# An FFN schedule that starts three stages later inside a Runge-Kutta scan

## The reference, cut to what matters

```
def _derivative(q, p, drive, coupling, bias):
    i_couple = jnp.tanh(q) @ coupling.T
    dq = q - q ** 3 / 3.0 - p + drive + i_couple + bias
    dp = EPSILON * (q + ALPHA - BETA * p)
```

```
gate_up = jnp.einsum('bsh,oh->bso', x, w_gu)
h = jax.nn.silu(gate) * up
y = jnp.einsum('bsi,hi->bsh', h, w_down)
rms = jnp.sqrt(jnp.mean(y * y, axis=-1, keepdims=True) + EPS)
```

## Time and profile before

| | |
|---|---|
| median of 3 runs | 1503.43 us (1503.01 to 1503.76) |
| the profiled execution | 1503.53 us |
| its span in the trace | 1501.7 us |
| PE busy | 1429.6 us (95%) |
| PEld busy | 1399.2 us (93%) |
| DVE busy | 1449.4 us (97%) |
| ACT busy | 719.2 us (48%) |

### The profile page before, as it was taken

How to read it: one execution, slowest core, us unless ns; L and a number is a source line. 1 busy time by engine, 2 the same in 40 slices (tenths; PEclk the granted TensorE clock), 3 DMA queues, 4 the chain that set the end, 5 groups by cost and what they waited for, 6 DMA issues and landing times.

```text
span 1501.7 us, 90826 instructions
## 1 busy us (share of the span) xinstructions
PE 1429.6 (95%) x37025; PEld 1399.2 (93%) x37025; DVE 1449.4 (97%) x11277; ACT 719.2 (48%) x4836; POOL 12.5 (1%) x39
## 2 busy tenths in 40 slices
PE   2477999999999999999999999999999999999998
PEld 0366999999999999999999999999999999999998
DVE  6999999999999999999999999999999999999991
ACT  2144445445454554545455454555455555545541
POOL 0000000000000000000000000000000000000000
PEclk9999999999999999999999999999999999999999
DMA  9200000000000000000000000000000000000000
GB/s 222 50 7 14 4 8 7 9 20 4 25 4 22 7 6 23 4 25 4 22 8 5 24 4 25 4 22 8 4 25 4 25 4 22 8 4 25 4 22 22
DMA packets 11942, 28.41 MB, mean 19 GB/s; under 512 B 1537, under 2 KB 5889, under 8 KB 11393
## 3 DMA queue, kind: packets, MB, share of 16 engines
q1 hardware_dynamic: 11522, 22.60, 6.0%
HBM read 18.40 MB, written 4.19 MB: 15 GB/s over the span
## 4 chain that ended last, share of the span: by engine, by line
PE 88%; DVE 8%; issue 0%; ACT 0%; POOLq 0%; DVEq 0%; POOL 0%; ACTq 0%
PE scan_ps L538 51%; PE gu_ps L301 22%; PE y_ps L313 14%; DVE th L610 1%; DVE q_stage L648 1%; DVE with_q L604 1%; DVE q_sq L614 1%; DVE scan_ps L622 1%; DVE q_stage L646 1%; DVE q_cub L617 1%; DVE p_part L604 1%; DVE with_p L604 0%; DVE q_raw L648 0%; DVE q_raw L646 0%; DVE hist L633 0%
## 5 line engine op out<-in xcount | busy, mean ns | idle before, releaser
L538 PE MATMUL scan_ps<-th,wscan 128*128 128x32 f16 (+1 forms) x32768 | 1006.1, 175 | 31.4 <-ACT th L576 31.1
L538 PEld LDWEIGHTS scan_ps<-th,wscan 128*128 128x128 f16 x32768 | 924.6, 96 | 49.1 <-ACT th L576 40.0
L576 ACT ACTIVATE th<-q_stage 128x16 f16<-128x16 f32 x1536 | 318.7, 207 | 524.3 <-DVE q_stage L646 524.3
L301 PE MATMUL gu_ps<-hist,wffn 128*128 128x128 f32 x2816 | 503.1, 284 | 0.0
L301 PEld LDWEIGHTS gu_ps<-hist,wffn 128*128 128x128 f32 x2816 | 393.8, 192 | 0.0
L610 DVE TENSOR_TENSOR th<-t,th 128x16 f16<-128x16 f32 x2048 | 357.9, 175 | 0.4 <-ACT t L578 0.2
L313 PE MATMUL y_ps<-wffn,h 128*128 128x128 f32 x1408 | 323.6, 313 | 0.0
L578 ACT ACTIVATE t<-q_stage 128x16 f32<-128x16 f32 x1536 | 306.2, 199 | 0.0
L313 PEld LDWEIGHTS y_ps<-wffn,h 128*128 128x128 f32 x1408 | 209.5, 189 | 0.4 <-DVE h L329 0.4
L576 ACT ACTIVATE th<-q_raw 128x16 f16<-128x16 f32 x512 | 106.2, 208 | 202.1 <-DVE q_raw L646 174.8
L379 ACT ACTIVATE sum_r<-dr,constant 128x64 f32<-128x64 f32 x528 | 174.3, 333 | 18.1 <-DMA dr<-drive 18.1
(11 more groups left out here) (36 smaller groups left out, 554.8 us busy)
## 6 DMA issues: line engine op xcount, KB each, us to landing
raw<-packed SPq DMA_DIRECT2D x11, 768.0 KB, 11.6
dr<-drive SPq DMA_DIRECT2D x34, 128.0 KB, 2.7
xres<-x SPq DMA_DIRECT2D x16, 256.0 KB, 3.5
out<-osb SPq DMA_DIRECT2D x16, 256.0 KB, 2.9
coup<-coupling_t SPq DMA_DIRECT2D x1, 1024.0 KB, 13.0
sc<-scales SPq DMA_DIRECT2D x1, 33.0 KB
q_raw<-cond_t SPq DMA_DIRECT2D x1, 16.0 KB, 5.6
bias<-bias_t SPq DMA_DIRECT2D x1, 2.0 KB, 6.2
```

The lines of the kernel that those rows point to most:

```text
L301: i = nc.tensor.matmul(gu_ps[b][:, half * P:(half + 1) * P], wffn[:, u, j * P:(j + 1) * P], hist[1 - f.parity][:, kt].rearrange("p t b -> ...
L538: i = nc.tensor.matmul(to if both else to[:, 0], wscan[:, w, part, kt, cols], moving if both else moving[:, 0], start=first, stop=last, sk ...
L576: nc.scalar.activation(th[s % 2][:, c, 0, :], q[:, c, :], ACT.Tanh, scale=1.0 / S).then_inc(now.tanh_hi, 1)
```

## The change

One number changes, and with it every stage at which the FFN has a job:

```
-FFN_FIRST = 0
+FFN_FIRST = 3
```

## The result

| | before | after |
|---|---|---|
| median of 6 runs each | 1503.8 us (1503.01 to 1504.88) | 1509.86 us (1509.34 to 1510.46) |
| ratio, 95% interval | | 1.0041 (1.003 to 1.0052) |
| profiled span | 1501.7 us | 1508.6 us |

The change costs 6.1 us, twice the 3.0 that were forecast, and the time lies above the predicted range.

A forecast was written before the change was run, and what follows sets the result against it. DVE was taken to end boundaries with two products, TensorE those with three. Blocks +1.1, start +0.1 and tail +1.8 us made 3.0 to 3.1 on 1503.53: 1506.5 us, put at 1506.4 against the median, range 1505.3 to 1507.8.

The forecast's parts named there:

- the block's sum of 0.08 us: Over one block's boundaries: 0.59 us less at those with DVE jobs, 0.67 more at step ends, net 0.08 slower.
- boundary 24: Boundary with the output's first part, no longer under three products: forecast 1.48 us.
- the term of +1.1: The 14 blocks with the full pattern, each 0.08 us longer: +1.1 us in all.
- the start: Second block: its slow boundary moves to stage 3, three stages ahead take 1.37 us: +0.1 us.
- the roof: A boundary with three products, ended by TensorE at 1.53 us, under which DVE's extra job is free.
- full 0.22 us: Third product behind stage 3: TensorE's stretch grows by one whole product, 0.22 us, nothing hidden; boundary 1.55 us.
- three terms: Tail: leftover products +1.3 us, wait before the last FFN's first down product +0.3, less cover at the end +0.2.
- POOL's clearing: Semaphores cleared at stages 54 to 55, DVE asks at 60: hidden, with 5 stages, 7 us, of cover.
- Rival 1: Third product partly hidden behind stage 3: boundary 1.48 us, 3.9 us less, 1502.6, no change that can be told; 13%.
- rival 2: Third product free at step ends: boundaries 1.37 us, 1.42 for boundary 3; 9.5 us less, 1497; 4%.
- Rival 3: Lost cover costs less as DVE's operations spread over neighbouring stages: up to 0.15 us per block, 1504.5; 8%.
- Rival 4: Semaphore clearing comes after DVE's wait at stage 60, lengthening each block: 1510 us or more; 3%.

The follow-up runs named there:

- e1: Kernel before with only the third products moved, to stages 3, 19, 35, 51, FFN start unchanged: 1508.93 us, ratio 1.0015.
- second pair: Changed kernel and kernel before, unedited, run and profiled again on one chip: 1510.81 us against 1506.31, ratio 1.0031; spans 1507.7 and 1502.6.
- e3: FFN started at stage 3 as in the change, third products kept at 0, 16, 32, 48, against the kernel before: 1508.13 us, ratio 1.001.
- first pair: The original profiles of the kernel before and the changed kernel: spans 1501.7 and 1508.6 us.
- e6: Kernel before with its output in five parts of 240, 76, 60, 76, 60 columns: 1501.54 us against 1504.0, ratio 0.9986.
- a_shift16: Changed kernel with 16 small writes ahead of DVE's setup: 1508.79 us, ratio 1.0029 against the kernel before.
- e4: Kernel before with its output in five parts of 232, 100, 40, 100, 40 columns: 1504.68 us against 1506.46, ratio 0.9989.
- e5: Changed kernel with the third products one stage on, at 4, 20, 36, 52: 1509.13 us, ratio 1.0021 against the kernel before.

## Why the prediction was wrong

**What failed: the block's sum of 0.08 us.** It priced each boundary by the products and the DVE job inside it and took every boundary behind a third product at the price of its kind. The boundaries that trade places came out as summed: 0, 16, 32 and 48 together -0.625 us (forecast about -0.61 of them), 3, 19, 35 and 51 together +0.67 (forecast +0.67), and the parts of the output changed places with `h32` almost evenly, +0.11 and -0.10. What is missing is the after-effect on 4, 20, 36 and 52: against a boundary with the same job behind two products, 0.03, 0.025, 0.027 and 0.028, together 0.11 us per block, 1.5 us in 14. Against it stands boundary 24, priced 0.02 too high: 0.08 + 0.11 - 0.02 = 0.17, the measured block. Said in the other count: the prediction took 0.18 us for the third product at the end of a step, and from L648 to L648, where the next stage's work starts, it is 0.205. In the kernel before the third product's effect fell on boundaries 1, 17, 33 and 49, which never hold a DVE job and absorb it as boundary 4 does in `e1` (1.346 to 1.348 behind three products, 1.344 behind two after the change); moving it to the last stage of a step lays it on exactly those that do. The trace of before held the numbers for it (0.17 between the reduces ahead of `h32`, and the forecast's own reading that TensorE would now be late); I didn't follow the lateness into the next boundary. Measured, the term of +1.1 is 2.2 to 2.3.

**The term that wasn't there: stalls of DVE's instruction stream, +0.96 us.** With them 2.16 for the blocks, 1.87 for the tail and 0.12 for the start make the 5.1 of the second pair. The trace of before shows two such stalls, of which the prediction doesn't speak; it put this term at nothing. A forecast of their size wasn't to be had from two of them. That the change made them costlier is two things at once. Seven places stall in place of two, which is luck of the counts. And the roof over them is gone: the same seven cost 0.43 us in `e3`, with the third products at 0, 16, 32 and 48, and 1.39 without them; the two of before cost 0.43 with it and 0.66 in `e1`.

**What held.** The third product costs its full 0.22 us over TensorE's side and gives 1.55 at the end of a step; boundary 24 at 1.46 (I said 1.48, by 0.02 too much); the tail by its three terms, +1.83 and +1.87 for 1.8, with the new wait where it was said to be; the start, +0.12 on one chip (+0.45 in the first pair); POOL's clearing, which cost nothing. That weight loads start while a matmul still runs holds too (the second load of the first product in boundary 0 starts at 851.18, while its first matmul is recorded from 851.09 to 851.45). But the two times that the prediction gives for it don't show it: 851.07 is the first load of the FFN's products, and 851.84 is the first matmul of the next `couple`.

**The rivals.** Rival 1 (1.48, partly hidden) and rival 2 (1.37, free) fell with boundaries 3, 19, 35 and 51 at 1.545 to 1.548. Rival 3 (the lost roof costs less) fell: the roof's price was all there, and `e6` earns it from the other side. Rival 4 (late clearing) fell: nothing waits at stage 60. I gave no case in which the FFN job itself becomes dearer behind a late TensorE, though this makes half of the 2.1 us that the forecast lacks against the second pair; the stalls make the other half.

**How the parts divide.** The late FFN without the move of the third products is +1.7 (`e3`), the move without the late FFN +2.5 (`e1`); their sum, 4.2, lies below the measured 4.5 to 6.1, and the 1.0 of the stalls, which neither shows in full, is on that side. The medians of the kernel before differ by up to 2.7 us from group to group (1503.8 to 1506.46) and the intervals of `e1` and `e3` reach 1.4 us to either side, so this comparison is a coarse one; the boundaries carry the explanation.

## What to carry to other kernels

When two engines take turns in setting the end of a short step, price a moved piece of work in its own step and in the next one: an engine that arrives late passes its lateness on, and whether it shows is decided by the slack of the next step. Count the step from the operation on which the next one's work hangs: here the second reduce, and I counted from the first. Put the extra work of the engine that waits under the steps where the other one is late (the roof), and look for what can still be moved there; cutting the output to fit gained 2.5 us. A loss of 0.03 us in one step of sixteen is 1.5 us here, half of what the forecast had in all.

## What the runs showed of the hardware that was not expected

**Stalls of an instruction stream.** In single places DVE went on 0.07 to 0.35 us late, with "issue" as the reason in most of them, and two profiles of one kernel show the same places. In all twelve traces the rule is the same (third to fifteenth block, DVE's instructions counted from 0, waits for semaphores included). Every late instruction has a count of 128 x n + 63: 1471, 2367, 3263, 5055, 5951, 8639 and 9535 in the changed kernel, 7 x 128 = 896 apart or multiples of it, and 2239, 5567, 5823, 8255 and 9151 in `a_shift16`. And nearly every one of them has a wait for a semaphore 1 to 3 places ahead. There are 53 such places in the twelve traces, and 51 of them are late, by 0.30 to 0.35 us with the wait right ahead, mostly 0.15 with it two places ahead and 0.08 with three. Of the 722 other such counts two are late, the same one in `e4` and `e6`, with the wait four places ahead. At all other counts no instruction is late by more than 0.04, with a wait ahead of it or not. So it isn't the job and isn't the count alone, but a wait just ahead of one of these counts. The schedule decides which waits fall there, and moving every wait by a few places changes it.

Instructions are brought in while the kernel runs. The page of the profile after lists two DMA queues for them:

```profile
q8 instruction: 289, 4.73, 1.4%
q14 instruction: 131, 1.07, 0.2%
```

Behind each of the 53 late instructions a packet of 8 KB starts on q14, 0.65 to 0.97 us later; behind the other counts of this kind one does so in 63 of 722 cases. So the stalls go together with the supply of instructions. How a wait and the supply get into each other's way wasn't shown.

**The clock at the start.** The second block's slow boundaries, up to 1.89 us, lie where the first products of the FFN come: 0 and 1 in before, 3 to 5 after, 0 to 3 in `e1` (1.89 in 0 only). Within them the matmuls of the products follow one another at 0.213 us, later at 0.112. They end around the recorded grant of TensorE's clock, at 151.6 us in before, 159.3 and 159.4 in the two profiles of after, 151.7 to 156.9 in the others; yet the page's row of granted clock stands at 9 tenths or more from its first slice on, so here that row doesn't show the slow stretch. The second block takes 88.0 to 88.7 us (in `a_shift16`, the longest, with a stall of 0.35 in boundary 62).

**The pace of an execution.** In the profiles of `e1` to `e5` nearly all boundaries with an FFN are 2 to 3 ns longer than in the other seven, about 0.15 us per block, and 2 us in the span. The edits don't explain it: `e4` shows it and `e6`, which differs from it in the widths of the output's parts only, doesn't. The setup ahead of the scan takes 59.1 to 62.4 us. Both are reasons to compare boundary by boundary within one trace, and to read a difference of 2 us between two spans with care.
